# Output transposes of two attentions as 32x32 blocks on VectorE, and small norm steps moved to GpSimd

## The reference, cut to what matters

```
x = layernorm(x + self_attention(x))          # 16 heads of 16, rotary, causal
x = layernorm(x + cross_attention(x, ctx))    # 16 heads of 16, causal, key mask
x = layernorm(x + ffn(x))                     # rmsnorm(x) * gamma; light and heavy branch, 9 x 128 hidden
```

## Time and profile before

| | |
|---|---|
| median of 3 runs | 995.03 us (992.27 to 995.65) |
| the profiled execution | 991.54 us, span 989.8 us |
| mean granted TensorE clock | 0.966 |
| TensorE busy | 903.1 us, 91% |
| VectorE busy | 731.6 us, 74% |
| ScalarE, GpSimd busy | 495.7 and 498.5 us, 50% each |

### The profile page before, as it was taken

How to read it: one execution, slowest core, us unless ns; L and a number is a source line. 1 busy time by engine, 2 the same in 40 slices (tenths; PEclk the granted TensorE clock), 3 DMA queues, 4 the chain that set the end, 5 groups by cost and what they waited for, 6 DMA issues and landing times.

```text
span 989.8 us, 21917 instructions
## 1 busy us (share of the span) xinstructions
PE 903.1 (91%) x7904; PEld 707.7 (71%) x7904; DVE 731.6 (74%) x1842; ACT 495.7 (50%) x1063; POOL 498.5 (50%) x905
## 2 busy tenths in 40 slices
PE   3367888999999999999999999999999999898886
PEld 2335565787878787787878787877878787776676
DVE  7777678677878878877878788887777788574612
ACT  1132443646465555646475655546464655446342
POOL 6454464545555564645464655646455555243221
PEclk8669899999999999999999999999999999999998
DMA  3884091936657290927566381918465572804000
GB/s 108 122 167 67 20 134 22 125 38 98 77 65 109 39 135 10 130 39 108 67 87 88 49 125 25 129 25 120 54 95 81 66 97 37 127 3 76 13 1 22
DMA packets 79644, 74.24 MB, mean 75 GB/s; under 512 B 8592, under 2 KB 78896, under 8 KB 79536
## 3 DMA queue, kind: packets, MB, share of 16 engines
q1 hardware_dynamic: 75008, 68.11, 48.9%
q10 hardware_dynamic: 4528, 4.73, 1.9%
HBM read 17.49 MB, written 4.20 MB: 22 GB/s over the span
## 4 chain that ended last, share of the span: by engine, by line
PE 55%; DVE 20%; issue 8%; DMA 7%; SPq 4%; POOL 3%; ACT 2%; ACTq 0%; POOLq 0%; DVEq 0%
PE bank L359 52%; DVE mx L931 9%; DMA stk1k<-nat1k 4%; SPq L282 4%; POOL pr L1249 2%; PE bank L386 2%; DVE qn L1064 2%; ACT pr L763 1%; PE bank L585 1%; DVE x L1012 1%; DMA stk2k<-nat1k 1%; POOL rstd L1239 1%; DVE nat2q L914 1%; DVE nat2q L916 1%; DVE rest L907 1%
## 5 line engine op out<-in xcount | busy, mean ns | idle before, releaser
L763 ACT ACTIVATE pr<-bank 128x384 f32<-128x384 f32 x512 | 241.1, 502 | 194.3 <-PE bank L359 194.0
L931 DVE TENSOR_REDUCE mx<-bank 128x3 f32<-128x384 f32 x512 | 264.3, 550 | 81.8 <-PE bank L359 80.1
L1249 POOL TENSOR_SCALAR_AFFINE_SELECT pr<-pr 128x256 f32<-128x256 f32 x512 | 226.7, 454 | 184.5 <-ACT pr L763 181.6
L359 PE MATMUL bank<-cmaskb,idb 128*128 128x256 bf16 x512 | 144.4, 282 | 32.9 <-DMA stk2k<-nat1k 13.9
L359 PE MATMUL bank<-w,g 128*128 128x256 f32 x576 | 170.8, 389 | 1.1 <-ACT g L775 1.1
L775 ACT ACTIVATE g<-bank,b 128x256 f32<-128x256 f32 x144 | 68.2, 474 | 91.6 <-PE bank L359 91.3
L1273 POOL TENSOR_TENSOR xTlow<-xT,xThigh 128x512 fp32r<-128x512 f32 x16 | 20.7, 1297 | 149.4 <-ACT xThigh L699 149.4
L359 PEld LDWEIGHTS bank<-w,g 128*128 128x128 f32 x576 | 89.6, 190 | 5.2 <-ACT g L775 1.5
L359 PEld LDWEIGHTS bank<-cmaskb,idb 128*128 128x128 bf16 x512 | 50.2, 98 | 59.5 <-DVE mx L931 28.7
L359 PE MATMUL bank<-stk2k,stk2q 97*128 97x128 bf16 (+1 forms) x512 | 85.1, 253 | 0.0
L359 PE MATMUL bank<-stk1k,stk1q 97*128 97x128 bf16 (+1 forms) x512 | 82.3, 248 | 0.0
(11 more groups left out here) (159 smaller groups left out, 1870.8 us busy)
## 6 DMA issues: line engine op xcount, KB each, us to landing
stk1q<-nat1q SPq DMA_DIRECT2D x90, 128.0 KB, 4.3
stk1k<-nat1k SPq DMA_DIRECT2D x90, 128.0 KB, 6.6
stk2k<-nat2k SPq DMA_DIRECT2D x90, 128.0 KB, 4.5
stk2q<-nat2q SPq DMA_DIRECT2D x90, 128.0 KB, 6.0
xT<-in_xT SPq DMA_DIRECT2D x16, 256.0 KB, 7.6
ctxT<-in_ctxT SPq DMA_DIRECT2D x16, 256.0 KB, 7.7
x<-in_x SPq DMA_DIRECT2D x16, 256.0 KB, 6.2
out_x<-x SPq DMA_DIRECT2D x16, 256.0 KB, 5.8
```

The source lines that it names most:

```text
L359: return nc.tensor.matmul(out, lhsT, rhs, start=start, stop=stop, skip_group_check=check)
L763: nc.scalar.activation(pr[:, h % (2 * HG), :], ring_bank("T", a, b, h)[:, 0:3 * P], ACT.Exp, scale=HD ** -0.5)\
L931: V.tensor_reduce(mx3[:, h, :], scored[:, 0:3 * P].rearrange("p (k t) -> p k t", k=3), AX.X, ALU.max, negate=True).then_inc(s_mx[a], 1)
L1249: G.affine_select(out=slot, in_=slot, compare_op=ALU.is_ge, fill=0.0, base=0, pattern=[[0, 2], [1, P]], channel_multiplier=-1).then_inc(s_ ...
```

## The change

- **Attention output.** `out_tokens`, `out_dims` and `copy_out` are gone. `normalise_pair(a, b, pair)` on VectorE takes two groups of four heads (`oT`, 128x512): a transpose of each 32x32 block into `tok`, a reciprocal, a multiplication and a second block transpose of 128x256 into `onT`. Since the blocks leave the dimensions in another order, the rows of `wo1` and `wo2` are put in that order on the host. Per attention and batch there are two pairs.
- **Where the pairs stand.** Of self-attention both are beside T2, before and behind `take_rest`. Of cross-attention pair 0 stands at the end of VectorE's step, behind the last Newton step, and pair 1 at head 5 of the next S1.
- **Norms.** The addition of epsilon moves from VectorE into GpSimd's `inverse_deviation`; `norm2` becomes GpSimd's `inverse_norm2`, right behind it and ahead of `mask_probs(1, s)` (the power of `rr2` stood at head 5 there). The third norm's last step runs on GpSimd a step later (`layer_norm3(i-4)`), ahead of the second norm's; of the last batch it stays on VectorE. The factor 16 of the rmsnorm goes into a constant.
- **Order.** On TensorE `out_proj` of f goes from head 12 to 11 of S1, that of s from head 10 to 9 of T2, where it follows the second `qk1`. On SP the store of the output goes behind the two `maxima` loads. Waits follow the new owners of the PSUM banks.

```diff
+            def normalise_pair(a, b, pair):
+                n = C * b + pair + 1
+                groups = slice(PG * pair, PG * (pair + 1))
+                dve.wait_ge(s_oT[a], NG * b + PG * (pair + 1))
...
+                V.transpose(tok[:, groups, :].rearrange("p g t -> p (g t)"),
+                            oT[:, groups, :].rearrange("p g t -> p (g t)")).then_inc(s_tok[a], 1)
+                dve.wait_ge(s_tok[a], n)
+                o = tok[:, groups, :].rearrange("p g (k w) -> p g k w", w=VW)
+                V.reciprocal(rden[a][:, groups, :], o[:, :, :, HD]).then_inc(s_rd[a], 1)
+                dve.wait_ge(s_rd[a], n)
+                V.tensor_tensor(on[:, pair, :].rearrange("p (k g d) -> p g k d", g=PG, d=HD), o[:, :, :, 0:HD],
+                                rden[a][:, groups, :].rearrange("p g (k o) -> p g k o", o=1)
+                                .to_broadcast([P, PG, NB, HD]), ALU.mult).then_inc(s_on[a], 1)
+                dve.wait_ge(s_on[a], n)
+                wait(dve, s_o[a], b)
+                V.transpose(onT[a][:, pair, :], on[:, pair, :]).then_inc(s_onT[a], 1)
...
                 if live(s):
+                    normalise_pair(1, s, 0)
                     take_rest(2, s, 1, 0)
-                    normalise_heads(1, s)
+                    normalise_pair(1, s, 1)
                     split_rest(2, s, 1, 0)
-                if live(l):
+                if l == B - 1:
                     layer_norm(3, l)
...
                     newton(i + 2, 1)
                     newton(i + 2, 2)
+                if live(c):
+                    normalise_pair(2, c, 0)
...
+            def inverse_deviation(a, b):
+                pool.wait_ge(s_mv[a], TT * (b + 1))
+                wait(pool, s_rs[a], b)
+                G.tensor_scalar(ve[a][:, :], mv[a][:, :, 1], LN_EPS, None, ALU.add).then_inc(s_ve[a], 1)
+                power(rstd[a][:, :], ve[a][:, :], s_rs[a], s_ve[a], b)
...
+            def layer_norm3(b):
+                pool.wait_ge(s_mv[3], TT * (b + 1))
+                G.tensor_scalar(nmean3[:, :], mv[3][:, :, 0], -1.0, None, ALU.mult).then_inc(s_nm3, 1)
...
+                for t in range(TT):
+                    G.tensor_scalar(xo[3][:, t, :], y[3][:, t, :], nmean3[:, t:t + 1], rstd[3][:, t:t + 1],
+                                    ALU.add, ALU.mult).then_inc(s_x[3], 1)
...
+                if live(i - 4) and i - 4 < B - 1:
+                    layer_norm3(i - 4)
                 if live(f):
-                    power(rstd[2][:, :], ve[2][:, :], s_rs[2], s_ve[2], f)
...
+                    inverse_deviation(2, f)
+                    inverse_norm2(f)
...
-X1T_AT, OUT2_AT, Q2_AT = 1, (3, 5, 10, 12), 4
+X1T_AT, OUT2_AT, Q2_AT = 1, (3, 11), 4
-K2_AT, OUT1_AT, QK1_AT, V1_AT = 1, (3, 4, 8, 10), (3, 9), 13
+K2_AT, OUT1_AT, QK1_AT, V1_AT = 1, (3, 9), (3, 9), 13
```

More of the change, by code:

```diff
@@ L339, in step @@
                     maxima(2, c)
+                if live(i - 4):
+                    sp.wait_ge(s_x[3], TT * (i - 3))
+                    load(tokens(io["out"], i - 4), xo[3][:, :, :], s_out)
                 if live(i + 1):
@@ L552, in values @@
                 last.then_inc(s_pv[a], 1)
[L554 to L593, removed]
             def out_proj(a, b):
@@ L597, in out_proj @@
                     pe.wait_ge(s_wcross, 16 * N_CROSS)
-                pe.wait_ge(s_onT[a], b + 1)
+                if a == 1:
+                    if live(b + 1):
+                        pe.wait_ge(s_rest[1], 2 * (b + 2))
+                    else:
+                        pe.wait_ge(s_rest[2], 2 * b)
+                else:
+                    if live(b + 3):
+                        pe.wait_ge(s_qn, TT * (b + 4))
+                    else:
+                        wait(pe, s_xnT, b)
+                pe.wait_ge(s_onT[a], C * (b + 1))
                 for t in range(TT):
@@ L634, in step @@
                 if live(f):
-                    add(OUT2_AT[1], out_tokens, 2, f)
-                    add(OUT2_AT[2], out_dims, 2, f)
-                    add(OUT2_AT[3], out_proj, 2, f)
+                    add(OUT2_AT[1], out_proj, 2, f)
                 if live(l):
@@ L709, in copy_dims @@
                 return copy(dst[:, :, :], bank[k][:, :].rearrange("p (c t) -> p c t", c=C))
[L711 to L715, removed]
             def copy_group(a, b, gr):
                 act.wait_ge(s_pv[a], NG * b + gr + 1)
[L720 to L724, removed]
+                pair = gr // PG
+                if a == 1 and live(b - 2):
+                    act.wait_ge(s_tok[2], C * (b - 2) + pair + 1)
+                elif a == 1 and live(b - 1):
+                    act.wait_ge(s_tok[1], C * (b - 1) + pair + 1)
+                elif a == 2 and live(b + 1):
+                    act.wait_ge(s_tok[1], C * (b + 1) + pair + 1)
+                elif a == 2:
+                    act.wait_ge(s_tok[2], C * (b - 1) + pair + 1)
                 copy(oT[:, gr, :], bank[OT_BANK][:, 0:T]).then_inc(s_oT[a], 1)
@@ L962, in max_t @@
                 V.tensor_copy(mT[a][:, :], bankb[MAX_BANK[a]][0:3 * H, 0:T]).then_inc(s_mT[a], 1)
[L964 to L977, removed]
+            def normalise_pair(a, b, pair):
+                n = C * b + pair + 1
+                groups = slice(PG * pair, PG * (pair + 1))
+                dve.wait_ge(s_oT[a], NG * b + PG * (pair + 1))
+                if a == 1 and live(b - 2):
+                    dve.wait_ge(s_on[2], n - 2 * C)
+                    dve.wait_ge(s_onT[2], n - 2 * C)
+                elif a == 1 and live(b - 1):
+                    dve.wait_ge(s_on[1], n - C)
+                    dve.wait_ge(s_onT[1], n - C)
+                elif a == 2 and live(b + 1):
+                    dve.wait_ge(s_on[1], n + C)
+                    dve.wait_ge(s_onT[1], n + C)
+                elif a == 2:
+                    dve.wait_ge(s_on[2], n - C)
+                    dve.wait_ge(s_onT[2], n - C)
+                V.transpose(tok[:, groups, :].rearrange("p g t -> p (g t)"),
[10 more added lines that the diff above has]
+                V.transpose(onT[a][:, pair, :], on[:, pair, :]).then_inc(s_onT[a], 1)
@@ L1141, in step @@
                     layer_norm(2, f)
-                    norm2(f)
                 if live(c):
@@ L1233, in rows, with inverse_norm2 @@
                 pool.wait_ge(s_rows, count + 3)
+            def inverse_deviation(a, b):
[3 more added lines that the diff above has]
+                power(rstd[a][:, :], ve[a][:, :], s_rs[a], s_ve[a], b)
+            def inverse_norm2(b):
+                pool.wait_ge(s_rs[2], b + 1)
+                wait(pool, s_ss2, b)
+                G.tensor_tensor(part2[:, :], mv[2][:, :, 1], rstd[2][:, :], ALU.mult).then_inc(s_p2, 1)
+                pool.wait_ge(s_p2, b + 1)
+                wait(pool, s_ssm, b)
+                G.tensor_tensor(ss2[:, :], part2[:, :], rstd[2][:, :], ALU.mult).then_inc(s_ss2, 1)
+                pool.wait_ge(s_ss2, b + 1)
+                wait(pool, s_sc2, b)
+                G.tensor_scalar(ssm[:, :], ss2[:, :], 1e-24 / D, None, ALU.max).then_inc(s_ssm, 1)
+                wait(pool, s_xn, TT * b)
+                power(rr2[:, :], ssm[:, :], s_sc2, s_ssm, b)
             def power(out, base, done, ready, b):
@@ L1370, in by_pairs, with by_blocks @@
         return w.reshape(D, HC, C, HD).transpose(0, 2, 3, 1).reshape(D, D)
+    def by_blocks(w):
+        return w.reshape(C, PG, HG, HD, D).transpose(0, 2, 1, 3, 4).reshape(D, D)
     arrays = {
```

88 lines of the change are left out of this document (34 added, 54 removed).

## The result

The changed kernel takes 1040.57 us (median of 4, 1037.45 to 1045.62) against 995.18 us (median of 4) for the kernel before: ratio 1.0467, 95% interval 1.0421 to 1.0514. The forecast was 1030 with a range of 1003 to 1058. The profiled execution took 1039.87 us with a span of 1038.1, against 991.54 and 989.8. TensorE's busy time fell from 903.1 to 885.6 us (85% of the span), VectorE's rose from 731.6 to 766.7 (74%), GpSimd's from 498.5 to 546.2 (53%), ScalarE's fell from 495.7 to 475.2.

The account below looks back on a forecast made before the run. VectorE, gapless for 10.6 us of each step up to a maximum in S1, was taken as the bound beside an equally full TensorE. Terms of 2.76 us per step, 14 times, less 2 at the ends, gave 1030 us (1003 to 1058).

Parts of the forecast that it names:

- A: First norm: later since the second square waits behind out_proj in T2 and epsilon is on GpSimd; +0.85 us per step.
- B: Cross-attention's pair 0 on VectorE, ahead of S1's first maximum, lengthens the gapless stretch; +1.7 us per step.
- C: Cross-attention's pair 1 at head 5 of S1 replaces the shorter normalise_heads on VectorE; +0.45 us per step (0.1 to 0.65).
- D: Four removed out_dims matmuls, late in S1 where TensorE sets the pace, save their time; -0.44 us per step.
- E: GpSimd's added norm work delays T1's first mask by 1.5 us; little reaches TensorE, +0.2 us per step (0 to 0.9).
- the signs it named: TensorE waits at head 3, head 9 and transpose_x1; pair 0 directly ahead of the first maximum; second square behind out_proj.
- At the ends: Where S1's maxima are absent, the removed matmuls lie on the path a few times: -2 us in all.
- rival 3: TensorE's clock falls after its waits in S1: +1.8 us per step, 1055 us if in all steps; chance 0.20.
- likeliest case: The forecast itself for the whole kernel: 1030 us, own range 1020 to 1040; chance 0.43.

Follow-up runs that it names:

- experiment 1: Changed kernel with out_proj of self-attention back at head 10 of T2, so the second square comes ahead of it: 1018.9 us, ratio 1.0241.
- experiment 2: Kernel before with only out_proj of self-attention moved from head 10 to head 9 of T2: 1021.05 us, ratio 1.0262.
- experiment 5: Changed kernel with cross-attention's pairs at heads 8 and 11 of S1, behind the split, and its out_proj at head 15: 1016.9 us, ratio 1.0220.
- experiment 6: Changed kernel with the edits of experiment 1 and experiment 5 together: 996.3 us, ratio 1.0020.
- experiment 8: Experiment 6's kernel with the second Newton step ahead of the first norm's last step and the norms as in the kernel before: 987.8 us, ratio 0.9938.
- e3: The run of experiment 5: changed kernel with cross pairs at heads 8 and 11 of S1, their out_proj at head 15: 1016.9 us, ratio 1.0220.
- e12: e3 with both cross-attention pairs at head 8 instead of heads 8 and 11: 1036.4 us, ratio 1.0390.
- e2: Changed kernel with pair 0 of cross-attention moved to head 5 of S1, right ahead of pair 1, out_proj left at head 11: 1082.0 us, ratio 1.0901.

## Why the prediction was right

Each step, against the profiled step that starts T2 at 647.08 (503.90 before):

| term | forecast | measured | read from |
|---|---|---|---|
| A, first norm | +0.85 | +0.91 | `x` at 662.77, 519.59 on the old scale, against 518.68 |
| B, pair 0 | +1.7 | +1.82 | first maximum 2.73 late, less A |
| C, pair 1 | +0.45 | +0.55 | head 9 of S1 3.28 late (675.80), less A and B |
| D, four matmuls | -0.44 | -0.23 | start of S2 3.05 late |
| E, masks in T1 | +0.2 | +0.10 | S2 and T1 21.94 against 21.84 us |
| step | 57.8 | 58.16 | |

The measured terms are successive delays along one chain, so they add up to the step by themselves; what speaks for the forecast is that each is near its own number and that the signs it named are there. The sum is 3.15 us against 2.76, 44 us over 14 steps against 38.6. At the ends I had 2 us of gain; the first step with all four phases starts at 81.6 us where it started at 84.5, which is 3. That leaves 7 of the profiled 48.3, and three S1 in which the clock fell come to as much: those from 190, 252 and 486 us took 24.4, 22.5 and 22.9 us at a mean clock of 0.79, 0.92 and 0.93 (the third is in the first fence), where the eight at 1.00 between 311 and 858 us take 20.5 to 21.5, in the mean 20.9. A fourth, from 546 us, had 0.92 and took 20.8. That is rival 3; it happened, but in a few steps only, and I had given it all or nothing. The result is just above the likeliest case's own range of 1020 to 1040; my sum was 1031.5, put down as 1030.

*Term A* holds in every link: head 9 of T2 1.0 late (forecast 1.14), the square at 657.92 likewise, the first norm 0.91. Experiments 1 and 2 show the cause by itself. What I did not see is its full weight: undoing it brings more than it cost, as the removed matmuls could have moved the first norm ahead by 0.4 (experiment 1).

*Terms B and C*: a pair is 1.86 us in its place against 1.7. The block transposes are 0.70 and 0.45 us where I took 0.62 and 0.38 from the reduction; both are above my upper bounds (0.68 and 0.43), if by 0.02. The streaming estimate that I worked out from the Trainium skill's "Vector Engine (DVE) Microarchitecture Reference" (The reshape front-end and per-opcode configuration), 0.53 and 0.27, is some 0.17 below both; the measurement decides. Pair 1 is longer than pair 0, 2.21 us, because of its multiplication (changed kernel, VectorE in time order: the first is pair 0's, the second pair 1's):

```profile
666.24 0.42 DVE L946 TENSOR_TENSOR on<-tok,rden 128x256 f32<-128x256 f32 x1
...
671.63 0.78 DVE L946 TENSOR_TENSOR on<-tok,rden 128x256 f32<-128x256 f32 x1
```

The second runs beside GpSimd's rotary work. The trace agrees with the rule of the Trainium skill's "GPSIMD Engine Reference" (Key points) that the two engines share SBUF interfaces, and the 0.36 us is near the 0.4 that I had named for it and not put into the sum; no run tries it by itself. That C came out only 0.1 above its forecast is luck: in this step pair 1 costs 1.00 us more than the two divisions that it replaces (2.21 against 1.21), over twice the forecast, and the split behind it gave 0.38 back, as its cast fell from 0.78 to 0.45. GpSimd's rotary work goes on beside that cast too (673.68 for 1.05 us), so why it is faster stays open, and the cast of the earlier trace rows was weak evidence for the rule.

*Term D* is half of its size, and the trace shows where the rest went. Behind head 9 the four matmuls of `out_dims` had filled the time until the next maximum; now the weight load of head 10 waits for it (changed kernel, TensorE's weight loads in time order):

```profile
676.26 0.09 PEld L360 LDWEIGHTS bank<-cmaskb,idb 128*128 128x128 bf16 x1 [0.24 <-DVE mx L890]
```

Head 10 starts 0.46 us behind head 9 where it was 0.72: 0.26 saved and not 0.44. That TensorE sets the pace from head 9 on was true only one head later. *Term E*: the first mask of T1 is at 697.53, 1.7 later against T1's start than before (forecast 1.5), GpSimd works eight off back to back in 3.67 us, and TensorE sees 0.1, as argued.

*What failed was my reading of where the gain would be without the loss* (experiments 5 and 6, not the forecast). I had counted TensorE's saved time as there to be had, once VectorE's pairs stood elsewhere. It is not: in experiment 8's kernel, the best of these, T2 ends in a wait for the stack's load in each of 13 steps, and S1 has 27 waits for maxima.

## What to carry to other kernels

Before work is moved off the busiest engine, cut the span by stage and look for the stretch where the receiving engine is full as well: here the same block transpose cost its full length ahead of the first maximum and nothing beside T2. An engine that loses work gains only what the next limit of each stage leaves: 24 matmuls, 42 us, gave 7 at best. When a wait had to stay, two short ones in different places beat a long one here (e3 against e12), in time and in TensorE's clock.

## What the runs showed of the hardware

Pauses of TensorE in the middle of a long kernel can halve its clock on the return. After a wait of 2.32 or 2.33 us for a maximum the granted clock fell to 0.50 in six S1 of e12 and stayed at 1.00 in five (from 192 us on); in e2, where one of 1.4 to 1.6 us stands just ahead of a wait of 2.3 to 2.9, the clock fell in each of twelve. Shorter pauses can do it too: in e3 it fell near 593.4, behind two of 0.85 and 0.67 us, and behind two of 0.79 and 0.72 (the S1 from 477.8) it stayed. What decides it there stays open. Where it falls, its price depends on who sets the pace: in e3 the clock was 0.50 from 594 to 596, while VectorE was busy without a gap, and that S1 took 19.7 us beside 19.6 at full clock; in e12 it fell where TensorE sets the pace and VectorE waits (384 to 386), and S1 took 20.9 us and more instead of 20.1.
